# Base rows of the last two tiles gathered earlier, and the last tile finished by halves

## What is computed

```python
xn = _layernorm(x, axis=-1)
x = x + _L0_attn_ref(xn, ...) + _L0_ffn_ref(xn, ...)

def body(acc, expert):              # in _L0_ffn_ref, once for each of 8 experts
    W1e, b1e, W2e, b2e, me = expert
    xi = inputs * me[..., None]     # me: 1 where the token is the expert's and within its capacity
    h = jax.nn.gelu(xi @ W1e + b1e, approximate=False)
    return (acc + (h @ W2e + b2e), None)
```

## Time and profile before

| | us |
|---|---|
| median of 3 runs | 637.82 |
| the three runs | 636.33, 637.82, 639.37 |
| the profiled execution, device time | 639.68 |
| its span, first to last instruction | 637.8 |

### The profile page before, as it was taken

One profiled execution on the slowest core, in us unless ns is written; L12 is line 12 of the kernel. 1 busy time (PEld: TensorE's weight loads), 2 busy tenths in 40 slices (PEclk: granted clock), 3 DMA queues, 4 the chain that ended last, 5 costly groups with the idle time before them and its releaser, 6 DMA issues.

```text
span 637.8 us, 16452 instructions
## 1 busy us (share of the span) xinstructions
PE 585.2 (92%) x4597; PEld 496.7 (78%) x4598; DVE 431.1 (68%) x830; ACT 433.0 (68%) x783; POOL 460.0 (72%) x619
## 2 busy tenths in 40 slices
PE   2998868898979999999999999999999999999990
PEld 1565545566869998989898989898898989898880
DVE  5789898788978988875564645555555556455542
ACT  4877678746978977785757576666667575757540
POOL 1999887871055544887878888888888888888466
PEclk9887778877989999999999999999999999999995
DMA  8994776557221315422222211122111211211110
GB/s 309 410 388 136 260 227 180 192 193 264 99 71 32 109 35 160 136 64 67 68 78 77 76 58 58 49 74 72 61 56 53 74 45 55 73 53 34 49 48 13
DMA packets 33587, 72.63 MB, mean 114 GB/s; under 512 B 6519, under 2 KB 19088, under 8 KB 33552
## 3 DMA queue, kind: packets, MB, share of 16 engines
q1 hardware_dynamic: 21488, 46.67, 20.9%
q0 software_dynamic: 11232, 25.20, 13.1%
q10 hardware_dynamic: 832, 0.31, 0.2%
HBM read 50.64 MB, written 27.00 MB: 122 GB/s over the span
## 4 chain that ended last, share of the span: by engine, by line
PE 74%; DVE 10%; ACT 6%; issue 6%; POOL 2%; DMA 1%; ACTq 0%; DVEq 0%; SPq 0%; POOLq 0%
PE ps_bu L888 10%; PE ps_bu L889 10%; PE ps_bu L890 10%; PE ps_t L862 5%; PE ps_t L864 5%; PE ps_t L863 5%; PE ps_y L864 5%; PE ps_y L862 5%; PE ps_y L863 5%; PE ps_y L730 3%; ACT area L532 2%; PE ps_t L698 2%; PE ps_bu L716 2%; PE ps_num L844 1%; POOL out L468 1%
## 5 line engine op out<-in xcount | busy, mean ns | idle before, releaser
L1331 DVE SCALAR_TENSOR_TENSOR ring<-ring,h_scale 128x512 f16<-128x512 f32 x156 | 116.0, 751 | 138.1 <-ACT ring L658 137.3
L888 PE MATMUL ps_bu<-area,ring 128*128 x624 | 170.1, 273 | 0.4 <-issue 0.4
L889 PE MATMUL ps_bu<-area,ring 128*128 x624 | 170.1, 273 | 0.0
L890 PE MATMUL ps_bu<-area,ring 128*128 x624 | 170.1, 273 | 0.0
L658 ACT ACTIVATE ring<-ring,h_act 128x512 f16<-128x512 f32 x144 | 104.0, 722 | 27.1 <-ACT ring L650 27.1
L468 POOL DMA_INDIRECT out<-ring,idx_b x78 | 99.2, 1272 | 18.2 <-issue 13.5
L452 POOL DMA_INDIRECT work<-xn_rows,idx_x x70 | 87.2, 1245 | 24.8 <-issue 24.2
L650 ACT ACTIVATE ring<-ps_t,b1t,inv_in 128x256 f32<-128x256 f32 x156 | 78.5, 555 | 33.2 <-PE ps_t L864 27.9
L478 POOL DMA_INDIRECT work<-base_rows,idx_b x78 | 83.3, 1068 | 18.0 <-issue 16.4
L862 PE MATMUL ps_t<-work,area 128*128 128x256 f16 x312 | 85.1, 273 | 1.7 <-ACT work L560 1.7
L392 POOL TENSOR_TENSOR small<-ones 128x1 f32<-128x1 f32 x152 | 51.0, 335 | 48.5 <-DVE ring L1358 19.5
(11 more groups left out here) (276 smaller groups left out, 1064.8 us busy)
## 6 DMA issues: line engine op xcount, KB each, us to landing
ring<-L_ffn_W SPq DMA_DIRECT2D x14, 1024.0 KB, 6.3
xn_rows<-area SPq DMA_DIRECT2D x8, 1024.0 KB, 8.9
base_rows<-area SPq DMA_DIRECT2D x8, 1024.0 KB, 6.6
area<-L_attn_u SPq DMA_DIRECT2D x7, 1024.0 KB, 18.1
work<-L_ffn_W SPq DMA_DIRECT2D x3, 1024.0 KB, 6.5
area<-L_ffn_W SPq DMA_DIRECT2D x3, 1024.0 KB, 5.6
work<-base_rows,idx_b POOLq DMA_INDIRECT x78
out<-ring,idx_b POOLq DMA_INDIRECT x78
```

The source lines that it names most:

```text
L888: t.matmul(dst, hh, wh, start=(c == 0), stop=False)
L889: t.matmul(dst, hh, wl, start=False, stop=False)
L890: last = t.matmul(dst, hl, wh, start=False, stop=(c == C - 1))
L1331: v.scalar_tensor_tensor(out=hlo[p][:, cs], in0=h32[:, cs], scalar=h_scale[:, bass.ds(e, 1)], in1=hhi[p][:, cs], op0=ALU.mult, op1=ALU.sub ...
```

## The change

Three edits, all at the end of the tile loop.

The base rows of tiles 37 and 38 no longer go into `bg` behind scatters 35 and 36. A new function `last_base` gathers them into `xg[1]` and `xg[0]`, the buffers of the normalised rows, when PE has turned these two tiles (`f_xt`). It runs right behind the base gathers of tiles 34 and 35 and uses the indices that still stand in `idx_x`; the scatters of tiles 37 and 38 use them too.

On PE, `down` of tile 38 signals `f_half` after half 0, and writes half 1 to `ps_h[0]` in place of `ps_o[0]`.

On DVE, tile 38 is finished by halves: empty PSUM, mask and base rows, constant row, each over one half; each half signals `f_end`, and POOL scatters it behind a gate of its own.

```diff
+            def last_base(j, gate_no):
+
+                pool.wait_ge(s["f_xt"], j + 1)
+                gate(gate_no)
+                for h in range(2):
+                    g.indirect_dma_start(out=xg[j % 2][:, h * D:(h + 1) * D], out_offset=None, in_=base_dram,
+                                         in_offset=bass.IndirectOffsetOnAxis(
+                                             ap=idx_x[:, 2 * (j % 4) + h:2 * (j % 4) + h + 1], axis=0),
+                                         bounds_check=bound, oob_is_err=False).then_inc(s[f"gl{j % 2}"], 16)
+                return gate_no + 1
+
             def out_and_base(t_out, t_base, ro, rb, gate_no):
+                if isinstance(t_out, int) and t_out == NT - 1:
+                    for h in range(2):
+                        pool.wait_ge(s["f_end"], h + 1)
+                        gate(gate_no)
+                        gate_no = gate_no + 1
+                        g.indirect_dma_start(out=out_rows,
...
+                    return gate_no
...
-                if is_tile(t_base):
+                if is_tile(t_base) and not ending(t_base):
                     g.tensor_copy(idx_b[:, 2 * rb:2 * rb + 2], idx_all[:, bass.ds(t_base * 2, 2)]).then_inc(s["ib"], 1)
...
                 gates = step(m, m % 4, gates)
+                if NT <= m < NT + 2:
+                    gates = last_base(m - 2, gates)
...
                         dst = ps_o[p][:, h * D:(h + 1) * D]
+                        if h == 1 and isinstance(j, int) and j == NT - 1:
+
+                            dst = ps_h[0][:, 0:D]
...
+                    if h == 0 and isinstance(j, int) and j == NT - 1:
+                        last.then_inc(s["f_half"], 1)
...
-                dve.wait_ge(gb[p], k * 32 + 32)
+                if ending(j):
+                    dve.wait_ge(gl[p], 32)
+                else:
+                    dve.wait_ge(gb[p], k * 32 + 32)
+                rows = xg[p] if ending(j) else bg[p]
...
-            drained(NT - 1, 0)
-            result(NT - 1, 0, NT // 2)
+
+            es = [dve.value_load(tile_expert[0:1, bass.ds(NT - 1, 1)], min_val=0, max_val=E - 1)] * 2
+            dve.wait_ge(s["f_o"], NT - 2)
+            dve.wait_ge(gl[0], 32)
+            dve.wait_ge(sc[0], (NT // 2) * 32)
+            for h, hs_ in enumerate(halves):
+                if h == 0:
+                    dve.wait_ge(s["f_half"], 1)
+                else:
+                    dve.wait_ge(s["f_y"], NT)
+                link(v.scalar_tensor_tensor(out=yr[0][:, hs_], in0=ps_o[0][:, hs_] if h == 0 else ps_h[0][:, 0:D],
+                                            scalar=inv_out[:, bass.ds(es[h], 1)],
+                                            in1=g_bc[:, bass.ds(es[h] * D, D)], op0=ALU.mult, op1=ALU.subtract))
+                link(v.scalar_tensor_tensor(out=yr[0][:, hs_], in0=yr[0][:, hs_], scalar=mask_slot[:, 2 * NT - 2 + h:2 * NT - 1 + h],
+                                            in1=xg[0][:, hs_], op0=ALU.mult, op1=ALU.add))
+                v.tensor_tensor(og[0][:, hs_], yr[0][:, hs_], c_bc[:, :], ALU.add).then_inc(s["f_end"], 1)
```

More of the change, by code:

```diff
@@ L234, in moe_ssm_kernel @@
             "kept_ok", "kept_t", "kept_read", "slots_ok", "kept_inv", "mask_ok",
-            "gx0", "gx1", "gb0", "gb1", "sc0", "sc1", "ix", "ib", "gates", "cleared",
-            "f_xt", "f_xhi", "f_xlo", "f_h", "f_gelu", "f_hhi", "f_hfirst", "f_hlo", "f_y", "f_yr", "f_ym", "f_o")}
+            "gx0", "gx1", "gb0", "gb1", "gl0", "gl1", "sc0", "sc1", "ix", "ib", "gates", "cleared",
+            "f_xt", "f_xhi", "f_xlo", "f_h", "f_gelu", "f_hhi", "f_hfirst", "f_hlo", "f_y", "f_yr", "f_ym", "f_o", "f_half", "f_end")}
         def zero_out(i):
@@ L252, in every_q, with ending @@
             return x.rearrange("n (p q) -> n q p", q=Q)[:, q, :]
+        def ending(j):
+            return isinstance(j, int) and j >= NT - 2
         def unit(n):
@@ L457, in rows_in @@
                 return gate_no + (1 if direct else 2)
-            def out_and_base(t_out, t_base, ro, rb, gate_no):
+            def last_base(j, gate_no):
[7 more added lines that the diff above has]
+                return gate_no + 1
+            def out_and_base(t_out, t_base, ro, rb, gate_no):
+                if isinstance(t_out, int) and t_out == NT - 1:
[4 more added lines that the diff above has]
+                        g.indirect_dma_start(out=out_rows,
+                                             out_offset=bass.IndirectOffsetOnAxis(
+                                                 ap=(idx_x if ending(t_out) else idx_b)[:, 2 * ro + h:2 * ro + h + 1], axis=0),
+                                             in_=og[ro % 2][:, h * D:(h + 1) * D], in_offset=None,
+                                             bounds_check=bound, oob_is_err=False).then_inc(sc[ro % 2], 16)
+                    return gate_no
                 if is_tile(t_out):
@@ L469, in out_and_base @@
                                              out_offset=bass.IndirectOffsetOnAxis(
-                                                 ap=idx_b[:, 2 * ro + h:2 * ro + h + 1], axis=0),
+                                                 ap=(idx_x if ending(t_out) else idx_b)[:, 2 * ro + h:2 * ro + h + 1], axis=0),
                                              in_=og[ro % 2][:, h * D:(h + 1) * D], in_offset=None,
                                              bounds_check=bound, oob_is_err=False).then_inc(sc[ro % 2], 16)
-                if is_tile(t_base):
+                if is_tile(t_base) and not ending(t_base):
                     pool.wait_ge(s["ib"], t_base + 1)
@@ L1306, in out_scales @@
                 link(v.tensor_scalar(inv_out[:, e0:e1].bitcast(I32), t_, 23, None, ALU.logical_shift_left))
-            gb = [s["gb0"], s["gb1"]]
+            gb, gl = [s["gb0"], s["gb1"]], [s["gl0"], s["gl1"]]
             sc = [s["sc0"], s["sc1"]]
@@ L1348, in result @@
                 dve.wait_ge(s["f_yr"], j + 1)
-                dve.wait_ge(gb[p], k * 32 + 32)
+                if ending(j):
[3 more added lines that the diff above has]
+                rows = xg[p] if ending(j) else bg[p]
                 for h, hs_ in enumerate(halves):
                     last = v.scalar_tensor_tensor(out=yr[p][:, hs_], in0=yr[p][:, hs_],
-                                                  scalar=mask_slot[:, bass.ds(j * 2 + h, 1)], in1=bg[p][:, hs_],
+                                                  scalar=mask_slot[:, bass.ds(j * 2 + h, 1)], in1=rows[:, hs_],
                                                   op0=ALU.mult, op1=ALU.add)
```

## The result

| | before | changed |
|---|---|---|
| median, us | 638.17 (4 runs) | 633.18 (4 runs) |
| profiled execution, device time | 639.68 | 634.01 |
| its span | 637.8 | 632.1 |

The medians differ by 5.0 us, 0.8%. The ratio formed from the runs is 0.9909 with a 95% interval of 0.9884 to 0.9934, so the change is faster, by about 0.9%. The forecast was counted from a median of 637.82 us of three runs; a fourth run put it at 638.17. Timed once more beside other kernels, the change gave 633.52 us and a ratio of 0.9925 (0.9903 to 0.9947).

The account below looks back on a forecast made before the run. It took POOL's queue behind PE's last matmul as the bound. Its terms, -2.81 - 2.80 - 0.22 + 0.09 + 0.34 = -5.4 us, took the median from 637.82 to 632.4 us, range 630.9 to 634.9.

Parts of the forecast that it names:

- What bounds: Behind PE's last matmul: POOL's queue of scatters and base gathers, 17.16 us, sets the end; VectorE only waits for it.
- What leaves the queue: POOL's tail: two base gathers (-2.81, -2.80) and their index copies (-0.22) go, one gate (+0.09) comes.
- rival 3: Tail: GpSimd and VectorE working at once slow each other's scatters, up to +3.6 us, 641.5 us; chance 0.06.
- Company beside VectorE: POOL's new tail: two more scatters run beside VectorE work, each 0.17 us longer, +0.34 us together.
- Waits of POOL for VectorE: POOL's tail: VectorE delivers each tile before POOL asks, slack 0.9 us at tile 37 and 0.2 at tile 38.
- L: Tail: time from the end of a scatter's second instruction to VectorE going on, taken as 1.3 us, at most 4.9.
- Rival 1: Before tile 38: a scatter lands later than a gather, so VectorE's wait decides; 632.9 to 635.8 us; chance 0.15.
- estimate of 2.15: Landing time of a scatter in us by the Trainium skill's fixed DMA cost of some 2.0, giving 633.1 us.
- Cover: Loop: 12.1 us of POOL idle time hide the moved gathers, about 6.8 us of work; cost on the path 0.
- Rival 2: Loop: idle time too thin, moved gathers take 14.1 us against 12.1, gain only 3.4, 634.4 us; chance 0.13.
- the row at 594.55: Loop: ScalarE reads tile 38's transpose then, taken to show both moved gathers' waits for PE are met at once.
- Halves: Last tile: nothing overlaps PE; POOL only issues half 0 while VectorE does half 1, for one more gate, +0.09 us.

Follow-up runs that it names:

- unused gathers: Full change plus two pairs of base gathers that nobody reads, put back between the tail's scatters: 639.40 us, ratio to before 1.0015.
- bases only: Full change without the halves: base gathers of tiles 37 and 38 moved, last tile emptied, summed and scattered whole: 633.20 us, ratio to before 0.9927.
- own buffer: Full change with the last tile's sum written to the free base buffer, without the wait for scatter 36: 633.00 us, ratio to before 0.9915.
- one more pair: Full change with the early base gather of tile 37 done twice: 633.8 us (one run).
- two more: Full change with the early base gathers of tiles 37 and 38 both done twice: 637.37 us, ratio to before 0.9991.
- halves only: Full change with the base gathers of tiles 37 and 38 back between the scatters, last tile still by halves: 638.32 us, ratio to before 0.9990.
- sums earlier: Full change with VectorE summing tile 35 before splitting tile 38's hidden rows, and tile 36 before emptying tile 37: 630.55 us, ratio to before 0.9882.

## Why the prediction was right

It said 632.4 us, 5.4 less than before; measured were 633.18, the medians differ by 5.0 and the profiled tails by 5.36. Step by step:

- **What bounds:** POOL's queue behind PE, not VectorE's wait. Right, and shown by the unused gathers, which bring 5.68 us back (13.35 - 7.67).
- **What leaves the queue:** -2.81 - 2.80 - 0.22 + 0.09 = -5.74. Right: the changed profile has only scatters there. They are eight instructions, two for each of four tiles; the prediction counted seven, here and in rival 3, and the sum doesn't use that count.
- **Company beside VectorE:** priced at +0.34. Wrong in sign. In the stretch of POOL's tail the eight scatters took 8.63 us before and 8.07 after, -0.56. The long ones of before, 1.27 and 1.20, are gone rather than joined by others. What was wrong is where the company falls, more than its price: VectorE idles 2.59 us from the second half of scatter 36 on, and scatter 37 took 1.00 and 0.97; where VectorE works beside it, it took 1.13 and 1.12 ("bases only") or 1.12 and 1.05 (own buffer).
- **Waits of POOL for VectorE:** priced at 0, with a slack of 0.9 and 0.2 us at two places. Measured 0.31 + 0.54 = 0.85. The 0.31 stands ahead of scatter 36, where the count had a slack of 0.04: it comes from scatter 35 being 0.25 shorter than in my count, while tile 36 was summed no earlier. The 0.54 has two parts. Counted from the gate of scatter 35, POOL was through with scatter 37 after 8.53 us, 0.38 earlier than in my count (8.91), since the scatters were shorter; and half 0 was summed after 8.98, 0.30 later (8.68), for the most part by L, below. That uses up the slack of 0.23, and 0.09 more pass from the end of the sum to the gate.
- The two misses nearly cancel: -5.74 - 0.56 + 0.85 = -5.45, and a gate of 0.36 in place of 0.22 brings it to -5.31, against 11.79 - 17.16 = -5.37 measured. The mechanism was right, but that the sum came out to 0.1 us is luck in two terms of opposite sign. They are not independent, though: a POOL that is faster runs into VectorE, so part of the shorter scatters came back as waits.
- **L, the landing of a scatter:** taken as 1.3. A full one, ended at 617.66 + 1.02 = 618.68, let DVE go at 620.21: 1.53. The half full one, ended at 621.84, let DVE go at 623.49: 1.65. The chain puts its landing at 623.15, so 1.31, and 0.34 lie between the landing and VectorE's first product: two waits (L1470, L1473) and the instruction that computes addresses for tile 38 (L1476). The rows of that (chain of the changed kernel: start, length, what):

```profile
620.87 2.28 DMA out<-ring,idx_b
623.15 0.03 issue
623.17 0.02 DVEq L1470
623.20 0.05 issue
623.24 0.05 DVEq L1473
623.29 0.05 issue
623.34 0.09 DVEq L1476
```

The prediction's L ran until DVE went on. By that it was too small by 0.35 us at the place that decides, though the landing alone was 1.31. In "bases only" the same scatter, ended at 620.05, let the last sum go at 621.46: 1.41, with no address work behind the wait. So the work behind the wait is worth 0.24 of the 0.34. Rival 1 was true in small. By the prediction's own sign (POOL's gate for half 0 waits for DVE, and DVE for a DMA to out) it holds, for 0.54 us of idle time; without the wait the tail was only 0.18 shorter. Its larger prices (L from 1.98 to 4.9) did not come about. Its estimate of 2.15 is near the whole way from the start of the issue to the landing, 2.28 us in the first row above, which has the issue's own 0.97 in it; L begins behind that.
- **Cover:** right. The idle time before the two places went from 2.53 and 5.24 to 0 and 0.73, and the tail paid nothing. The moved pairs with their gates took 3.3 and 3.6 us, 6.9 in all, as the count beside a busy DVE (6.8) had it. PE paid nothing either: from the sum of tile 0 to PE's last matmul it is 374.59 us before and 374.51 to 374.58 in the eleven other profiles. The experiment with one more pair shows that some 4 us more would still have been free, that with two more where it ends. Rival 2 is out. One reading was loose: the row at 594.55 is tile 38's turn, 6 us ahead of the second place and behind the start of the first. The first needs tile 37's, which ScalarE reads at 583.63. Neither gather waited.
- **Halves:** predicted to bring nothing, at +0.09. They cost 0.31 net, because they also pull VectorE's work behind the wait for scatter 36.
- **Rival 3** (POOL slowed by VectorE): no scatter of the new tail took over 1.07 us. Out.

## What to carry to other kernels

When a wait in the tail names a transfer, look at the engine that issued it: if its queue has no idle time, the transfer is late because of the queue, and what helps is a shorter list there, not an earlier request by itself. Work that can be moved in front of such a tail is free up to the idle time of the same engine in the loop, and each us beyond it is paid in full. Splitting the last item pays only when the consumer of the halves waits for them, and a wait belongs right ahead of the instruction that needs it, not ahead of the block.

One limit: with this input tiles 37 and 38 hold no token, so their gathers and scatters moved nothing. What the tail would be with full tiles at its end, no run shows.

## What the runs showed of the hardware

A scatter's issue on POOL ended 0.14 to 0.17 us behind the end of VectorE's sum in four cases of the tail where it took 1.20 us or more: before 619.30 behind 619.15 (duration 1.27) and 630.72 behind 630.58 (1.20); with the halves only 618.39 behind 618.24 (1.27); with the unused gathers 619.80 behind 619.63 (1.28). In the changed kernel the same scatter stands about 0.1 us earlier against that sum, and took 1.02, ending at 618.68, before the sum's end at 618.90. So 0.1 us of phase went with 0.25 us. That fits a port which one of the two engines holds for a whole instruction, as the Trainium skill has it (SBUF — State Buffer, section "SBUF: two separate sides"); no run varied the phase by itself, so the cause is argued and not shown. Nor is 0.15 us the whole rule. Other long issues ended 0.85 to 0.91 us behind the end of a VectorE instruction: with the sums earlier, that of 1.44 us at 612.08 behind 611.17; with the bases only, that of 1.12 at 623.00 behind 622.15. Which part of an issue is held stays open.

An indirect DMA whose slots are all empty costs POOL as much as a full one: the scatters of tile 38 took 1.00 us each in the changed kernel and wrote nothing (0 GB/s from 625.0 to 628.5 us), and those of tile 35, full ones (in the kernel before 101 GB/s over 618.2 to 619.5 us and 94 over 619.5 to 620.9, 131 KB each), took 1.04 and 1.02. The window from 626.4 us to past POOL's end in the kernel before (columns as in the earlier trace rows) holds the second half of the base gather of tile 38 and the scatters of 37 and 38:

```profile
626.40:633.80 7.40, 0.00 (x0) 0.00 (x0) 1.57 (x3) 0.00 (x0) 5.72 (x8) 0.50 0.02 0
```

POOL was busy 5.72 of 7.40 us, and 0 GB/s were moved.

The part before the tile loop, not the loop, carries the spread between executions. Tile 0 was summed at 245.58 us in one profile of the changed kernel and at 242.82 in the other, 2.76 apart, and the last matmul is 2.75 apart, at 620.09 and 617.34:

```profile
245.58 0.69 DVE L1395 TENSOR_TENSOR ring<-ring,c_bc 128x512 f32<-128x512 f32 x1
```

```profile
242.82 0.69 DVE L1395 TENSOR_TENSOR ring<-ring,c_bc 128x512 f32<-128x512 f32 x1
```

(Timelines of DVE, first and second profile of the changed kernel.) That is why a change of 0.3 us could be read from a tail and not from a median.
